# Another merge of five instruction streams, with 392 filler matmuls in place of 329, in a decoder layer in fp32

## The chip, the cores and the metric

The kernel runs on one NeuronCore of a Trainium2 chip. The metric is the device time of one execution in microseconds (us), as the median of several runs. One further execution was recorded by the hardware profiler; all rows below are from that one. Engines are named as the profile names them: PE is TensorE, DVE VectorE, ACT ScalarE, POOL GpSimd and SP SyncE. SP computes nothing here, it issues most of the DMAs.

## What is computed

Input `x` is 4 sequences of 512 tokens with 512 channels. Three residual blocks follow one another, each on a layer norm of its input:

```python
x = x + attention(layernorm(x), ...)                 # 16 query heads of 32, one shared key/value head, causal
x = x + quantised_mlp(layernorm(x), fside, ctx)      # two int8 "smooth quant" products with a silu gate between
x = x + ffn(layernorm(x), ...)                       # DFF 1376, shared LoRA, and 8 experts of LoRA rank 8, top 2 per token
```

The second block scales activations and weights by column maxima, rounds both to integers, multiplies, and undoes the scales; the first product is 512x512x512, the second 512x256x512. The third has a gate, an up and a down product. Accurate fp32 products are made of three matmuls on a high and a low part of each operand.

## The kernel before, in words

The work is cut into steps. Each step has a name and a place, such as `("max", b, g, i)`, where `b` is the sequence (0 to 3). Five generators list the steps in five streams:

- **A**, attention (`attention_steps`, from line 136): `turn1` transposes the normalised input; `kv`, `q` and `v` project; `rows` turns the row maxima of four heads; `scores`, `values`, `sums` and `context` are the softmax and its product with v; `out` projects.
- **X** (`maxima_steps`): 44 `max` groups for each sequence. PE computes scores with a causal mask into a PSUM bank (L1126 the mask, L1129 the scores), DVE reduces them to the negative row maximum (L1409). Groups 0 to 10 of four heads are: one of 4 heads x 128 columns, two of 2 x 256, four of 1 x 384, four of 1 x 512.
- **L** (`layer_steps`): the quantised block and the layer norms around it. DVE takes column maxima (L1459, L1474), scales (L1506), and takes row maxima (L1512); POOL scales the weights (L803); PE transposes and multiplies.
- **F** (`feed_forward_steps`): `turn3`, `low_in`, `router`, and then for each of 11 column tiles `gate`, `up`, `hid`, and by segments of tiles `ad` and `down`. It is the largest part of PE's work: L1056, L1057 and L1058 are the three matmuls of an accurate product.
- **W** (`preparation_steps`): once at the start, the shared LoRA is folded into the weights of the third block, tile by tile. `prep_gu` multiplies a fold of 8 rows on PE (L1066), DVE adds it (L1357), ACT rounds to the high part (L849), POOL takes the low part (L730); `prep_dn` is the same for the down weights (L1073, L1364, L855, L735). `prep_out(f)` on SP stores tile f and loads the raw weights of tile f+2 (L586 to L592). `gu_first` and the first `dn_load` fetch the prepared tiles, when all are stored.

A string, `TURNS`, merges the streams: each letter takes the next step of that stream, and a digit n is a `fill` of n matmuls. Inside a stream the order is fixed; only the merge is free. Every engine, SP among them, walks through the same merged list and issues its own part of each step (`for name, *where in ORDER`). So the order in the list is the order on all five queues, and each of them is strictly in order: an instruction that waits holds back all that is behind it on its queue. SP's queue carries, in the order of the list, the 8 + 1 transfers of each `q` step (L638, L642), the two transfers of each `rows` step (L649), which bring the row maxima to where `scores` reads them, the stores and loads of `prep_out`, and the loads of weights (`w_load`, L676: the weights of the quantised block).

A fill does no useful work:

```python
def fill(n):
    ps = in_ring.upcoming(pe)
    for _ in range(n):
        pe.matmul(ps[:, 0:2 * P], ident_bf[:, 0, :], ident_bf[:, :, :].to_broadcast([P, 2, P]), start=True, stop=True, ...)
```

It multiplies 128x128 by 128x256 in bf16 (L1053) into the one of the two `ring` banks that is to be used next, when that is free, and nobody reads the result. Banks of PSUM are handed out in the order of the list (`tenants_of`), four of them in rotation as `slots` and two as `ring`.

Of the kernel before, what the change touches and what calls it, by code (L numbers as in the profile page):

```python
# [303 lines left out]


TURNS = (
    "AAAAAAAAA6AAAAAAWAAX2X1WX9XXXXAXXXXXXAXWXXX3XWXXXW6XX91AXAAXXAAAXXAAAA1AAWXAAWXAAAAAW4A2AWXWXX5AWXXXAAAXXAXXXA"
    "XXAAAAAAAWXAAAAWAAAAAA79AAAAWAAAWAAA4AAAAAWAAAWAAAAAAA99AAAAAAAAAWAAAWAAAAAAAALALA2L5ALWLLLL5AWALAALLLWL15XXXX"
    "93LL1XXLXXLLLXLLLAXAWLXL995AWXXXXLXLLL9AAAXXXX4XLLLLXXAALXLLLWXXLLL31ALLALAXWAALXXL8AALAAAA1XW9LLLWXLAALAAAXL8"
    "XLAAXLAAALAL9AAXAAAXLLXLAAX94XLLLWLLWLLAWLLLAALXAXLXXLXAAAAAA2W8ALAAAAAAWALLLAAAAALWAALLAAWAAF6FALAAAAFAAAFAAA"  # L310
    "ALFWWWALAFAAALLLFAFAAFALLAALAFFAFFFFLAALLAFAAFFFXFXFLXLXXFLFFFFFFFLXFXAFFXXXFFFXXXFFFLFFFFFFFLXXFFLLLXLFXFF2FF"
    "FFAFFFFFLFFLFLXFXALLLFAFLXFXXFFALLFFLFFXAXLLLAXFFLFFXFALFFFLAFFLFFAFLFFFLLFLFLFXFLLLLAFFFLLXFFAFAALFLFFFFLAAXF"
    "FXXFXXFFLAFAXXFFFFFFFAXFALLFFLFFXFXXFLFFXFFFAFFLFAALLFAFFAAFLAFFFFLLAFAFAFFFFAAAAAALAFLFLAFAXFXFLLFXLAALFAFFAL"
    "AFLFAFLXAFLLLFFAFALFFAFFAALLFLAAFLAAFFFAFAFFLFFAAFLALFALFFALFFFFAAAAAFFLAAFFAAAAAFAAFAAAAFFFFLLAAFAFLAFFLAAAFF"
    "LLFLLFFFFFFFAFFFFFFAALFFFFLAAFFALAAFXFXXFFXXFLFFLFXFFXXFFFLFXXXFXAFFXXAFFFXFFLLLFFFFAFFFAXXFFFLLLFFFXXFFXXFFXL"
    "FFXFFXLLFLAFLXLLLFXAFFFFFAFFFLFLALFLAAAAFAALLFXFFFFLAALFLALFLAALAAFAAALFXFLLFLFFLFLFLLXFXLFFFFLLFFFLFFFFFFFLFF"
    "FLFLXLFFFLFLLXLLXAAFLFXFFFLFFFLLFFFFAFLXFXFXFLLFFXFFFXLFXFLFLFFFFLLXLFFFLFALLLFAFAALFFAXAFFXFFFAALLLFALFXFFLFF"
    "ALLLLFFAAAFFAFFFFAAAFAAFLLLFFFLFAAAFFFFFFFFAFFAAFFFAAFFFAAAAAAFFAAAAFAFFFAAAFAFLLLFAAFAAAAAFFAFAAFFFAAFAFAFAAF"
    "FAFFAFFFFFFFFFAFFFFFLLFFLFFLFFFLFFFLLFLFFFF9FFFLLFLF4LLFFFFFLFLFFFLFFLFFLFFFLLLFFFFLFFFLFFFLFFFLLFFLLFFFFFLLLL"
    "FFFFLFLLFFFLLFFLFFLFLFFFLLLFFFLFLFFFFFFFFLFLLFFFFLFLFLLLFFFFLLFLFFFFFLLFFFFFLFLFFLFFFLFFLLFLLFFFFLFLLLLFLFFFFF"  # L320
    "FFFFFLFFLLFLFFFFLFFFLFLLLLFFFFFFFFFFFFFFFFFFFFFFFF4F94F5FFFFF7FFFFFFFFFFFFFFFFFFFFFFFFFF994FFFFFFFFFFFFFFFFFFF"
    "F94FFFFFFFFFFFFFFFFFFFFFFFFFFFFFFFFFFFFFFFFFFFFFLFFFFFFFFFFFFFFFFF94FFFFFFFFFFFFFFFFFFFFFFFFFFFFFFFLFFFFFFFFF9"
    "FFL4FFFFFFFFFFFFFFFFFFFFFFFFFFFFFFFFFFFFFFFFFFFFFFFLFFFLFFFFFF2FFFFFFFFF")
# [1405 lines left out]
```

How the kernel before makes its waits and increments, by code:

```python
    def __call__(self, ins):  # L60
        self.n += 1
        ins.then_inc(self.chain.sem, 1)
        self.eng.wait_ge(self.chain.sem, self.chain.at(self.b, self.n))
# [11 lines left out]
    def claim(self, eng, key, signal, value):  # L75
        first, width = bank_after(self.next, BANK_WIDTH.get(key[0], 1))
        assert self.table[key] == (first, width), key
        for bank in range(first, first + width):
            if bank in self.left and (bank == first or self.left[bank] != self.left[first]):
                eng.wait_ge(*self.left[bank])
        for bank in range(first, first + width):
            self.left[bank] = (signal.sem, value)
        self.next = first + width
        return self.banks[:, first:first + width, :]
# [8 lines left out]
    def claim(self, eng, key, signal, value):  # L93
        place = self.n % 2
        self.n += 1
        assert self.table[key] == place, key
        if place in self.left:
            eng.wait_ge(*self.left[place])
        self.left[place] = (signal.sem, value)
        return self.places[place]
# [1 line left out]
    def upcoming(self, eng):  # L102
        place = self.n % 2
        if place in self.left:
            eng.wait_ge(*self.left[place])
        return self.places[place]
# [472 lines left out]
            def prep_wo():  # L580
                sp.wait_ge(wo_lo.sem, KT)
                sp.dma_start(wo_parts, wo_first[:, :, :].bitcast(F32)).then_inc(wo_stored.sem, 16)
# [29 lines left out]
            def x_load(b):  # L612
                if b < BATCH:
                    sp.wait_ge(xT_ps.sem, xT_ps.at(b - 1, 2))
                    if b > 1:
```

## Time and profile before

| | |
|---|---|
| median of 3 runs | 943.83 us (941.45 to 944.6) |
| the profiled execution's own time | 943.11 us |
| its span from the first to the last instruction | 941.4 us |
| PE busy | 902.0 us, 96% of the span |
| DVE, ACT, POOL busy | 552.4, 338.5, 309.5 us |
| mean granted clock of TensorE | 0.976 of full speed |

A busy PE is not a PE at its peak: a fill counts as busy, and so does a matmul at half the clock. The granted clock is 1.00 when TensorE runs at 2.4 GHz and 0.50 at 1.2 GHz. The idle time before an instruction stands behind it with the instruction that ended it; idle time on an engine that is not the bound costs nothing.

### The profile page before, as it was taken

How to read it: one execution, taken by the hardware profiler on the slowest of the kernel's cores; microseconds unless marked ns; L12 is line 12 of the kernel's file. 1: busy time of each engine (PE TensorE's matmuls, PEld its weight loads, DVE VectorE, ACT ScalarE, POOL GpSimd, SP SyncE). 2: the span in 40 equal slices, each digit the busy share in tenths (PEclk: the TensorE clock that was granted, in tenths of full speed). 3: DMA queues.
4: the chain of work that ended last, by engine and by line, in shares of the span. 5: the costliest groups of instructions: out<-in, count | busy, mean ns of one | idle time of the engine just before them, and what ended most of it. 6: DMA issues, size and time to landing. Idle time of an engine off the chain costs nothing.

```text
span 941.4 us, 13548 instructions
## 1 busy us (share of the span) xinstructions
PE 902.0 (96%) x5191; PEld 667.7 (71%) x5191; DVE 552.4 (59%) x897; ACT 338.5 (36%) x577; POOL 309.5 (33%) x419
## 2 busy tenths in 40 slices
PE   3989998899999999999999999999999999999998
PEld 2756567655578886766688767766778778688886
...
GB/s 310 266 207 256 301 190 129 171 142 211 307 224 175 218 129 150 130 201 240 117 174 251 134 106 161 132 290 108 163 159 162 168 180 206 91 242 194 170 179 95
DMA packets 44964, 175.07 MB, mean 186 GB/s; under 512 B 7196, under 2 KB 10268, under 8 KB 34916
## 3 DMA queue, kind: packets, MB, share of 16 engines
...
## 4 chain that ended last, share of the span: by engine, by line
PE 84%; DVE 7%; SPq 3%; ACT 2%; issue 2%; DMA 2%; POOL 0%; ACTq 0%; DVEq 0%
PE ring L1056 13%; PE ring L1058 13%; PE ring L1057 13%; PE slots L1129 4%; PE slots L1146 4%; PE av L1164 4%; PE ring L1296 4%; PE den L1164 3%; PE slots L1056 3%; PE slots L1058 3%; PE slots L1057 3%; SPq L642 2%; PE slots L1233 2%; PE ring L1053 2%; PE slots L1126 2%
## 5 line engine op out<-in xcount | busy, mean ns | idle before, releaser
L815 POOL TENSOR_TENSOR hd_l<-hd,hd_h 128x512 fp32r<-128x512 f32 x44 | 58.3, 1324 | 298.3 <-ACT hd_h L1023 298.3
L1056 PE MATMUL ring<-xT_h,gu 128*128 128x512 f32 x352 | 142.2, 404 | 0.0
L1058 PE MATMUL ring<-xT_h,gu 128*128 128x512 f32 x352 | 137.6, 391 | 0.0
L1057 PE MATMUL ring<-xT_l,gu 128*128 128x512 f32 x352 | 137.6, 391 | 0.0
L1409 DVE TENSOR_REDUCE negm<-slots 128x1 f32<-128x384 f32 (+3 forms) x176 | 106.4, 636 | 43.5 <-PE slots L1129 42.0
L931 ACT ACTIVATE probs<-slots 128x512 f32<-128x512 f32 (+1 forms) x176 | 90.0, 560 | 91.5 <-PE slots L1146 91.2
L782 POOL TENSOR_SCALAR_AFFINE_SELECT probs<-probs 128x128 f32<-128x128 f32 (+2 forms) x176 | 61.9, 361 | 132.7 <-ACT probs L931 130.7
L1129 PE MATMUL slots<-kst,qst 97*128 97x128 f32 (+3 forms) x256 | 77.7, 374 | 0.0
L1056 PEld LDWEIGHTS ring<-xT_h,gu 128*128 128x128 f32 x352 | 66.3, 188 | 15.2 <-issue 3.3
L1019 ACT ACTIVATE gated<-ring 128x512 f32<-128x512 f32 x44 | 26.3, 597 | 140.1 <-PE ring L1296 136.2
L1058 PEld LDWEIGHTS ring<-xT_h,gu 128*128 128x128 f32 x352 | 66.1, 188 | 14.5
L1057 PEld LDWEIGHTS ring<-xT_l,gu 128*128 128x128 f32 x352 | 66.4, 189 | 11.5
L1651 DVE TENSOR_TENSOR total<-ring,total 128x512 f32<-128x512 f32 x60 | 41.1, 687 | 48.1 <-PE ring L1058 47.6
L1146 PE MATMUL slots<-qst,kst 99*128 99x512 f32 (+1 forms) x176 | 63.0, 425 | 6.2 <-DMA qst<-negm_hl 4.5
L1056 PE MATMUL ring<-dn,hd_h 128*128 128x512 f32 x168 | 67.4, 401 | 0.9 <-DVE total L1651 0.9
L1057 PE MATMUL ring<-dn,hd_h 128*128 128x512 f32 x168 | 65.6, 391 | 0.0
L1058 PE MATMUL ring<-dn,hd_l 128*128 128x512 f32 x168 | 65.6, 390 | 0.0
L1023 ACT ACTIVATE hd_h<-hd 128x512 fp32r<-128x512 f32 x44 | 27.8, 631 | 100.3 <-DVE hd L1617 100.1
L1606 DVE SCALAR_TENSOR_TENSOR gated<-gated,ring 128x512 f32<-128x512 f32 x44 | 30.0, 683 | 53.6 <-ACT gated L1019 53.5
L1617 DVE SCALAR_TENSOR_TENSOR hd<-gated,ring 128x512 f32<-128x512 f32 x44 | 30.2, 686 | 47.8 <-PE ring L1296 39.2
L1126 PE MATMUL slots<-mask_r 128*128 128x128 f32 (+2 forms) x176 | 52.0, 295 | 2.0 <-DMA qst<-qT_h 1.5
L1129 PEld LDWEIGHTS slots<-kst,qst 97*128 97x128 f32 x256 | 49.1, 213 | 4.8
...
## 6 DMA issues: line engine op xcount, KB each, us to landing
...
qst<-qT_h SPq DMA_DIRECT2D x128, 64.0 KB, 2.1
...
```

The lines of the kernel that those rows point to most:

```text
L782: pool.affine_select(probs[:, at:at + heads, 0:P], probs[:, at:at + heads, 0:P], [[0, heads], [1, P]], ALU.is_ge, 0.0, base=0, channel_mul ...
L815: pool.tensor_tensor(hd_l[:, i, :], hd[:, i, :], hd_h[:, i, :].bitcast(F32), ALU.subtract).then_inc(hd_lo.sem, 1)
L931: act.activation(probs[:, at:at + heads, 0:n], slot("scores", b, step, unit)[:, 0, 0:heads * n].rearrange("p (h n) -> p h n", n=n), ACT.Ex ...
L1056: pe.matmul(out_, w_hi_, m_hi_, start=start, stop=False, skip_group_check=True)
L1057: pe.matmul(out_, w_hi_, m_lo_, start=False, stop=False, skip_group_check=True)
L1058: return pe.matmul(out_, w_lo_, m_hi_, start=False, stop=stop, skip_group_check=True)
L1126: pe.matmul(diagonal, mask_r[:, 0, :], mask_r[:, 1:2, :].to_broadcast([P, heads, P]), start=True, stop=False, skip_group_check=True)
L1129: mm = pe.matmul(ps[:, 0, h * n:(h + 1) * n], qst[0:MROW, 4 * g + h0 + h, qt * P:(qt + 1) * P], kst[0:MROW, 0:n], start=False, stop=True, ...
L1146: pe.matmul(ps[:, 0, 0:heads * n].rearrange("p (h n) -> p h n", n=n), kst[0:MROW + 2, kt * P:(kt + 1) * P], qst[0:MROW + 2, 4 * g + h0:4 * ...
L1164: mm = pe.matmul(to[HD * c:HD * c + HD, kt * P:T], weights, probs[:, 4 * (step % 2) + c, 0:n], start=(kt == TT - 1), stop=(kt == 0), skip_ ...
L1409: dve.tensor_reduce(negm[:, h0:h0 + heads, qt], slot("max", b, g, i)[:, 0, 0:heads * n].rearrange("p (h n) -> p h n", n=n), AX.X, ALU.max, ...
L1651: dve.tensor_tensor(total[:, tt, :], ps, total[:, tt, :], ALU.add)\
```

## The change

Only the string is another. All 1772 steps stay, each stream keeps its own order, and every engine issues the same instructions except for the fills. The digits sum to 392 in place of 329, so 63 matmuls are added. The list as it stands in the program, cut to the part in which the first two sequences go through attention and the preparation is made (the lines that follow are changed in the same manner):

```diff
 TURNS = (
-    "AAAAAAAAA6AAAAAAWAAX2X1WX9XXXXAXXXXXXAXWXXX3XWXXXW6XX91AXAAXXAAAXXAAAA1AAWXAAWXAAAAAW4A2AWXWXX5AWXXXAAAXXAXXXA"
-    "XXAAAAAAAWXAAAAWAAAAAA79AAAAWAAAWAAA4AAAAAWAAAWAAAAAAA99AAAAAAAAAWAAAWAAAAAAAALALA2L5ALWLLLL5AWALAALLLWL15XXXX"
-    "93LL1XXLXXLLLXLLLAXAWLXL995AWXXXXLXLLL9AAAXXXX4XLLLLXXAALXLLLWXXLLL31ALLALAXWAALXXL8AALAAAA1XW9LLLWXLAALAAAXL8"
-    "XLAAXLAAALAL9AAXAAAXLLXLAAX94XLLLWLLWLLAWLLLAALXAXLXXLXAAAAAA2W8ALAAAAAAWALLLAAAAALWAALLAAWAAF6FALAAAAFAAAFAAA"
-    "ALFWWWALAFAAALLLFAFAAFALLAALAFFAFFFFLAALLAFAAFFFXFXFLXLXXFLFFFFFFFLXFXAFFXXXFFFXXXFFFLFFFFFFFLXXFFLLLXLFXFF2FF"
...
+    "AAAA4AAAAA4AAA6AAA2AW2AAXX9XXXWXXXXX3XXX4AXWXXXWXXXXWXXXXXX991AXXAXAAAAAXWAAAAAAAAXAWAAAAAXAX92AAAAAXXAAAAAXXA"
+    "WXXWAAAAWAXXXAAWAAXA3A9AAAAAAAAAAWAAAAAWAAAAAAAAAAW8AAAAAWAAAAAAAWAWAAAAAAWWALA5LLA5AL5LWWWLLAALLA3ALLL94X2XX1"
+    "LWWXXLXLXLLWXXLLXAXLX24X5XLX1L423LLAAL5LLXL9XLL928X9X92L6XLAWXXLLXLWLWLL5AL3ALLXLXAAAAAALWAAAL3AXA5XAXAAWLLA1L"
+    "LXXL93X3AAAAX6LXXAALLALLALXAL5AAAALLAXAALWXXLL71LLLLAL2ALLLXLLX3WLLLALAWXLWLAALX6WAAXA5X5FAAAAAFAFAAAA3FAA4AAA"
+    "AAAAAAAFFAAAAAAAAAAALLAFALAWWWALALFLLAAAFLLAAFLAFAFFLLAAFFALAAFXFFXXXFXFFFXFXXFLFXFXFFFLLXFFFLFAFLXXFX1LFFFAFFF"
...
```

What it does between some marks, counted in the two lists (`scores(0,0,0)` is the first score step of the first sequence, `out(b,0)` the first half of a sequence's output projection, `product0(0,0)` the first product of its quantised block):

| from | to | fills before | fills after |
|---|---|---|---|
| start | `scores(0,0,0)` | 37 | 53 |
| `scores(0,0,0)` | `out(0,0)` | 50 | 31 |
| `out(0,0)` | `product0(0,0)` | 67 | 114 |
| `product0(0,0)` | `out(1,0)` | 68 | 79 |
| `out(1,0)` | end | 107 | 115 |

The same steps that use PE stand between these marks in both lists, but for three moves across them: `max(0,2,1)` to `max(0,2,4)` stand ahead of `scores(0,0,0)` after the change and behind it before; and a few steps cross `product0(0,0)`. Within the marks, `prep_gu(1)` to `prep_gu(4)` come later: `prep_gu(4)` has 11 `scores` steps, 6 `values` steps, `prep_dn(4)` and `prep_gu(5)` between it and `out(0,0)` before, and `values(0,14)`, `prep_dn(4)`, `values(0,15)` and `prep_gu(5)` after. `w_load(0)` follows `prep_out(4)` on SP's queue in both. `prep_gu(6)` and `prep_gu(7)` come earlier: `prep_gu(7)` stands between `scale_w(0,0,0)` and `scale_w(0,0,1)`, the first two of the four pieces in which POOL scales the weights, and stood behind `turn_w(0,0)`. `wqkv_out`, two stores of 1.15 MB each on SP's queue, moves from ahead of `q(0,2)` to behind it.

## Rows read from the trace of the kernel before

**Rows 1.** Stretches of the run, us: busy time of each engine, granted clock, DMA.

```profile
core 0: us, PE busy (x) PEld busy (x) DVE busy (x) ACT busy (x) POOL busy (x), PEclk, DMA share, GB/s
0.00:57.00 57.00, 37.64 (x196) 28.24 (x196) 24.32 (x43) 19.63 (x31) 26.07 (x33) 0.94 0.78 257
57.00:123.00 66.00, 64.15 (x491) 37.84 (x491) 32.77 (x61) 35.64 (x66) 38.30 (x67) 0.85 0.79 287
123.00:263.90 140.90, 132.50 (x919) 88.41 (x915) 107.13 (x174) 69.56 (x117) 70.78 (x96) 0.94 0.56 192
263.90:941.40 677.50, 667.69 (x3592) 513.25 (x3591) 388.18 (x620) 213.65 (x363) 174.30 (x224) 1.00 0.47 169
```

**Rows 2.** The same view of the two longest stretches at half clock.

```profile
49.66:63.31 13.65, 10.07 (x50) 7.97 (x51) 3.51 (x7) 2.53 (x6) 4.49 (x7) 0.50 0.54 195
76.97:90.62 13.65, 13.65 (x66) 9.63 (x68) 8.66 (x15) 5.11 (x10) 6.88 (x11) 0.50 0.60 210
```

**Rows 3.** PE in order of time: start, duration, engine, line, operation, count, idle before.

```profile
47.46 0.83 PE L1053 MATMUL ring<-ident_bf 128*128 128x256 bf16 x6
...
51.49 2.36 PE L1053 MATMUL ring<-ident_bf 128*128 128x256 bf16 x10
56.94 0.80 PE L1146 MATMUL slots<-qst,kst 99*128 99x512 f32 x1 [3.10 <-DMA qst<-negm_hl]
```

**Rows 4.** SP's queue in order of time, up to the first transfer of row maxima.

```profile
49.34 5.02 SPq L642 DMA_DIRECT2D qst<-qT_h  x8
54.47 1.15 SPq L649 DMA_DIRECT2D qst<-negm_hl  x2
```

**Rows 5.** PE in order of time: starts of two kinds of max groups, at full clock.

```profile
34.18 0.37 PE L1126 MATMUL slots<-mask_r 128*128 128x256 f32 x1
...
34.62 0.28 PE L1053 MATMUL ring<-ident_bf 128*128 128x256 bf16 x1
...
36.40 0.23 PE L1126 MATMUL slots<-mask_r 128*128 128x128 f32 x1
...
36.69 0.22 PE L1126 MATMUL slots<-mask_r 128*128 128x128 f32 x1
```

**Rows 6.** Fills: the shortest, median and longest, and 16 in a row at full clock.

```profile
L1053 PE MATMUL ring<-ident_bf x329: 272/273/437, 18.4 to 934.8; 128*128 128x256 bf16 x165
```

```profile
98.14 1.92 PE L1053 MATMUL ring<-ident_bf 128*128 128x256 bf16 x16
```

**Rows 7.** PE's waits over the whole run, the longest line: total, times, longest.

```profile
PE slots L1083 <- ACT x_in L860: 14.2, 4, 13.6
```

**Rows 8.** POOL and DVE in order of time: scaling of weights, scaling of activations, low parts.

```profile
161.45 6.97 POOL L803 TENSOR_TENSOR w_raw<-w_raw,rows 128x512 f32<-128x512 f32 x4 [2.63 <-ACT rows L946]
```

```profile
161.69 2.13 DVE L1506 TENSOR_TENSOR xn<-xn,rows 128x1024 f32<-128x1024 f32 x1
...
164.80 1.26 DVE L1506 TENSOR_TENSOR xn<-xn,rows 128x1024 f32<-128x1024 f32 x1
...
172.00 1.21 DVE L1512 TENSOR_REDUCE qm<-w_raw 128x2 f32<-128x1024 f32 x1
```

```profile
98.56 2.91 POOL L730 TENSOR_TENSOR gu<-raw_gu,gu 128x1280 fp32r<-128x1280 f32 x1 [2.53 <-ACT gu L849]
```

**Rows 9.** The load of the quantised block's weights: fold, values, projection, issue, landing, use.

```profile
105.61 1.16 PE L1066 MATMUL ring<-fold 8*128 8x128 f32 x16
```

```profile
119.83 0.85 PE L1164 MATMUL av<-probs,v 128*32 128x384 f32 x8
...
122.97 0.50 PE L1056 MATMUL slots<-wo_h,hT_h 128*128 128x512 f32 x1
```

```profile
116.16 1.31 SPq L676 DMA_DIRECT2D w_raw<-w  x1
```

```profile
w_raw<-w SPq DMA_DIRECT2D x1, 1024.0 KB, 9.0
```

```profile
140.03 3.94 DVE L1459 TENSOR_REDUCE tile_max<-w_raw 128x256 f32<-128x1024 f32 x2
```

More of the change, by code:

```diff
@@ L312 @@
[L312 to L321, printed above, removed]
@@ L322 @@
-    "F94FFFFFFFFFFFFFFFFFFFFFFFFFFFFFFFFFFFFFFFFFFFFFLFFFFFFFFFFFFFFFFF94FFFFFFFFFFFFFFFFFFFFFFFFFFFFFFFLFFFFFFFFF9"
-    "FFL4FFFFFFFFFFFFFFFFFFFFFFFFFFFFFFFFFFFFFFFFFFFFFFFLFFFLFFFFFF2FFFFFFFFF")
+    "AAAA4AAAAA4AAA6AAA2AW2AAXX9XXXWXXXXX3XXX4AXWXXXWXXXXWXXXXXX991AXXAXAAAAAXWAAAAAAAAXAWAAAAAXAX92AAAAAXXAAAAAXXA"
+    "WXXWAAAAWAXXXAAWAAXA3A9AAAAAAAAAAWAAAAAWAAAAAAAAAAW8AAAAAWAAAAAAAWAWAAAAAAWWALA5LLA5AL5LWWWLLAALLA3ALLL94X2XX1"
+    "LWWXXLXLXLLWXXLLXAXLX24X5XLX1L423LLAAL5LLXL9XLL928X9X92L6XLAWXXLLXLWLWLL5AL3ALLXLXAAAAAALWAAAL3AXA5XAXAAWLLA1L"
@@ new lines @@
+    "LXXL93X3AAAAX6LXXAALLALLALXAL5AAAALLAXAALWXXLL71LLLLAL2ALLLXLLX3WLLLALAWXLWLAALX6WAAXA5X5FAAAAAFAFAAAA3FAA4AAA"
+    "AAAAAAAFFAAAAAAAAAAALLAFALAWWWALALFLAAAFLLAAFLAFAFFLLAAFFALAAFXFFXXXFXFFFXFXXFLFXFXFFFLLXFFFLFAFLXXFX1LFFFAFFF"
+    "FFFFXXFLXFXFLFFLFFLFFFFFFFLFFFLFFLLLLFAFFLFAFLFFLXAFLXFXFLLFLLXFAXXFFFFFLFLFFFLFFFLXFLFXFFALLAFXFFFLLLFLFAALFL"
+    "ALFFLAFLLAAFFALAXFAXLLFLFFAXALAFLXXLFFAFFAFLFXFAFXFXFAFAFLFFFAFLXFXXXFXFFAFAAFFXAAAALLAFFFFAFFFFAAFFALAFAFXFXF"
+    "AFAAFLFLAFAFFLLFFLLLFFFXFLLFLLFLFAFLALAFAAALALFAAAFFFAFAFFLAALAAFFFFFFAFLFLAALFLFAFAFFFAAFLFFAAAAAAFFAAAAAAFFF"
@@ new lines @@
+    "FAAAALAFFFFFALALLFAFLFFFLLLFFFAFFFFFAFFFFFFFFAAFLLAAAFFXFXFXFXXFFXFLFLLXXAFFFLFXFXFXFFFXLLFFFFXFFXFFAXFFFFFXLX"
+    "FLFFLXLFFAFFFFLLLFAFFFLLLFFLLFXFLXFFFLFFLFLLFFFAFALFLFFLXLFXFFFFFALLFXFFXFLFFLFFAAXFLLLLFLLAFFFXFFFFLFLALLFAAF"
+    "ALFAAXFFALFAFLFXF1FFLLFFFLFFLLFLLAFXFFFLFFLXLLXFFFFFLFFFFFLLXFFFXLXFALFAAALLLFLFLFLALXFLFFAFXXXFFLFFAAFFAFAFLF"
+    "FFFLFFAXAAFFFFFLAAAAFXXFXAXLFXLLAAAFFFFFAFFAFAFAAAFAAAFFFFAFFAAAFAAFAAFALAAFAFAAAFFFAFAAAFAFFAAFAFAAAFFFAAAFLA"
+    "AAFAFAAAFFFLLLLLLLFFFAFFFFAFLFFFFALFFFFFFFFFLLFFLFF2LFFLFLFFFL92F3FFFLFLLFFFFFFLLLFFFLLFFFLFFLLFFFFLFFLFFFLFLF"
@@ L326, in streams_of @@
+    "FFLFFFFLFLLFLFFLFLFFFFLFFLFLFLLFFFLLFLLFFLFLFFLFLFFFFFFFLFFFFLFFLLFFFLFLFFLLLFLFFFFLFFLFFFLLFFLFFLFFFFFFFLLLFF"
+    "LLFLFFFFLLFFLLFFFFFFFLFFFFFFFFFFFLFFFFLFFFFFLFFLFFFFLFFFLLLFFLFFLFFFFFF92FFF8FF7FFFFFFFFFFFFFLFFFFFFFFFL4FFFF9"
+    "94FFFFFFFFFFFFF594LLFFFFFFFFFFFFFFFFFFFFFFFFFFFFFFFFFFFFFFFFFFFFFFFFFFFFFFFFF4FFFFFLLFFFF9FFFFFFFFFFFFFFFFFFFF"
+    "FFFFFFFFFFFFFFFFFFFFF9FFFFFFFFFFFFFFFFFFFFFFFFFFFFFFFFFFFFFFFFFFFFFFFFFFFFFFF4FFFFF1FFFFFFFFF")
 def streams_of():
```

## The prediction

> **What bounds the kernel now.** I read the run in stretches first [rows 1]. From 263.9 us on PE is busy for 667.7 of 677.5 us at full clock: that part is bound by PE's own work, which the change does not touch, and a merge can win almost nothing there. What can be won lies ahead of it, and I cut that at two marks of the list. Up to 57 us PE is busy for 37.6 us only. From there to `out(0,0)` at 123 us it is busy for 64.2 of 66.0 us, but at a mean clock of 0.85. From 123 to 263.9 us it is busy for 132.5 of 140.9 us at 0.94, while DVE is busy for 107.1.
>
> So I read the clock next. A clock of 0.85 over 66.0 us is 0.15 x 66.0 = 9.9 us of full-rate work not done; 0.94 over 140.9 us is 8.5 us; up to 57 us it is 0.06 x 57 = 3.4 us. Two stretches of 13.65 us each at 1.2 GHz hold most of it [rows 2]. The first has PE busy for 10.1 us of it, so waits lie inside. The second has it busy for all 13.65 us: there half a clock is half of the work, and nothing else shares the blame. Ahead of the first, TensorE had issued 6 fills and little else, then stood in a wait [rows 3]. The waits themselves are few: the longest line of them holds 14.2 us, and 13.6 of it are one wait at the start [rows 7]. The losses ahead of 263.9 us are thus fills, low clock and waits, in a part that is tied by dependencies.
>
> The mark at 57 us is fixed by SP, not by PE. `scores(0,0,0)` waited 3.10 us for a transfer of row maxima [rows 3]. SP issued it at 54.47 us, directly behind eight transfers of q that took 5.02 us to issue [rows 4]. The list after the change has the same transfers on SP's queue ahead of it, so I expect `scores(0,0,0)` at 57 us again, within 1 us; the two stores of `wqkv_out` change places with one `q` step, and all of them stay ahead of the row maxima.
>
> **The change, part by part.** I count against the profiled execution, 943.11 us with a span of 941.4 us; the median of the runs is 0.7 us above it.
>
> Work ahead of the fixed mark. Four max groups move in front of `scores(0,0,0)`, where PE only had fills and a wait. A group of two heads takes 34.62 - 34.18 = 0.44 us from start to start, one of a single head 36.69 - 36.40 = 0.29 us [rows 5]. Two of each are 1.46 us that no longer have to be done behind the mark: **-1.5 us**. The bound on the good side is twice that, when they would have run at half clock behind it; on the bad side 0, should the 19 fills that now stand between them and the scores be late: at half clock ten fills took 2.36 us [rows 3], so 19 can take 4.3 us, against 2.1 at full clock.
>
> The fills. One fill by itself takes 0.27 us, 16 take 1.92 us, so each further one costs (1.92 - 0.27)/15 = 0.11 us [rows 6]. The 63 are worth 6.9 us if nothing hides them. Their places matter more. Ahead of the first mark there are 16 more: they stand in the wait for SP, 0. Between the marks there are 19 fewer, 2.1 us; they too stood mostly in waits, which come back unless other work is ready, and I take 0. From `out(0,0)` to `out(1,0)` there are 58 more, 6.4 us. What would hide them is the chain of the quantised block, which runs through DVE, and PE's idle time of 140.9 - 132.5 = 8.4 us [rows 1]. I take 0, between +6.4 us (all in PE's way) and a gain of 8.5 us (they keep the clock up throughout); the busy DVE is the nearest row. From `out(1,0)` on there are 8 more in a part where PE is the bound: **+0.9 us**.
>
> The clock between the marks. 9.9 us are at stake [rows 1, 2]. The first low stretch began in the wait ahead of the mark; now five max groups and 19 fills keep PE issuing through that wait. The second stretch came in a mixture of thin prep folds, waits and few max groups; the folds of tiles 1 to 4 now stand later. They do not vanish, and with 19 fills fewer there the clock can fall at another place. I take 6 of the 9.9 us: **-6.0 us**, between 0 and -9.9. In the Trainium skill, TensorE: Matmul & The Clock Gate, section Terms, the penalty of throttled time is that time multiplied by the share of the clock that is missing. By that alone the term would be -9.9 us and the whole sum 3.9 us lower; I hold it for an upper end, because the first of the two stretches here contains waits that no clock shortens.
>
> POOL in the quantised block. `prep_gu(7)` now stands between the first and the second piece of POOL's scaling of the weights. Its low part takes 2.91 us [rows 8]. What is queued behind it on POOL are three scaling pieces, and DVE's row maxima of the weights wait for the last of them. In the trace POOL was done with all four at 161.45 + 6.97 = 168.4 us and DVE came to them at 172.0 [rows 8]: 3.6 us of slack, so 2.91 us fit, barely. But DVE multiplies the activations in the same place. That took 2.13 us while POOL was scaling, and 1.26 us the second time [rows 8]. I put **+1.0 us** for one more such collision on a busy DVE; its bounds are 0 and the 2.9 us for which POOL works. The Trainium skill, SBUF — State Buffer, section SBUF: two separate sides, says that a DVE operation with two inputs from SBUF and a GpSimd operation exclude each other for the whole instruction. By that rule the term would be 2.9 us and the sum 1.9 us higher; the row shows one multiplication longer by 0.87 us.
>
> The load of the weights. `prep_gu(4)` stood at 105.61 us, 17.4 us ahead of `out(0,0)`, and the load that follows its tile on SP was issued at 116.16 us, 10.6 us behind it [rows 9]. After the change `prep_gu(4)` itself, two `values` steps and two more folds lie between. The same two `values` steps took 122.97 - 119.83 = 3.1 us, and a fold 1.16 us [rows 9]: 3.1 + 3 x 1.16 = 6.6 us. The load is then issued 4 us behind the start of `out(0,0)` and, with 9.0 us to land, there at +13. DVE asked for it at 140.03, which is +17 [rows 9]. So 4 us of slack are left of 15; I charge 0, up to 3 us if the transfers of the tiles around it crowd it.
>
> Sum: -1.5 + 0.9 - 6.0 + 1.0 = **-5.6 us**. From the median of 943.83 us that is **938.2 us**. The steps after 263.9 us are merged in another order too; their waits in the trace are so small that I charge nothing for it, within 3 us either way.
>
> **The rivals.** A difference of 0.3%, 2.8 us, is about what a measurement of this kernel tells from none.
>
> First, the clock falls again. Nothing in the trace says that the new mixture between the marks is dense enough: the stretch that fell at 76.97 us was full of instructions, and the fills that could help are 19 fewer. Then -1.5 + 0.9 + 1.0 remains: 944.2 us, no difference. Against it stands the first stretch, whose cause is a plain wait that is now filled. Chance 0.18.
>
> Second, slower: the 58 fills between `out(0,0)` and `out(1,0)` are in PE's way. PE takes them in order, so a fill that starts when the chain's next matmul is ready delays the chain, then DVE, then the next sequence. It decides from the point at which less than their 6.4 us of PE's time there would have been idle. For it: 47 of them stand ahead of `product0(0,0)`, where DVE had hardly an idle gap; against it: PE's 8.4 us of idle time and 8.5 us of lost clock in that stretch [rows 1]. With the clock not regained between the marks it gives 944.2 + 6.4 = 950.6 us; with it, 944.6. The first is the rival: chance 0.26.
>
> Third, more than I take: both parts keep their clock. Then all 9.9 and 8.5 us are regained, with -1.5, +0.9 and +1.0: 943.83 - 18.0 = 925.8 us. It needs fills at every gap of the quantised block's chain, and DVE not to be the bound there, against 107.1 us of DVE in 140.9. Chance 0.10.
>
> That the change does not do what it says is no rival with a price: the fills are plain instructions and all of them are issued.
>
> **The numbers.** The forecast has 0.46: 938.2 us. The range reaches down to the third rival, with little behind it, and up to the second: 926 to 951 us. The forecast alone has 932 to 943. Faster by over 0.3% gets the forecast's larger part and the third rival, 0.52; within 0.3% the first rival and the forecast's upper end, 0.21; slower 0.27.
>
> **What would show it.** Right: the wait for the row maxima ends at 57 us within 1; `out(0,0)` starts between 114 and 118 us in place of 123; the mean clock between the marks is over 0.92; from `out(0,0)` to `out(1,0)` it takes 140 to 143 us; from there to the end 678 to 679. Wrong: a stretch of over 10 us at half clock behind 57 us (first rival); more than 146 us from `out(0,0)` to `out(1,0)` with PE busy throughout (second); a wait of DVE for the weights, or of the row maxima for POOL's scaling (my terms of POOL and of the load). If the time after `out(1,0)` differs by more than 3 us, what I left out of the sum was what mattered.

## The result, and the profile after

| | before | after |
|---|---|---|
| median (15 runs each, same chip) | 940.99 us (938.32 to 944.6) | 937.65 us (931.4 to 942.42) |
| ratio of the times, 95% interval | | 0.995 [0.9933, 0.9967] |
| profiled execution: its time, its span | 943.11, 941.4 us | 942.42, 940.7 us |
| PE busy | 902.0 us | 909.0 us |
| mean granted clock | 0.976 | 0.980 |

The change makes the kernel faster by 0.5%, 3.3 us between the medians. The profiled execution of after is the slowest of its 15, and its mean clock is one of the two lowest: the 15 lie between 0.980 (942.42 us) and 0.992 (934.47 us), and the fastest two, 931.4 and 931.74 us, had 0.989 and 0.991. Of one and the same list, how long TensorE stays at half clock differs between executions, so a stretch of one profile is a single sample.

The same stretches as in [rows 1], between the same marks, which now stand at 58.1, 110.8 and 258.9 us (columns as there), and behind them the longest stretch at half clock:

```profile
0.00:58.10 58.10, 45.15 (x222) 33.40 (x222) 26.64 (x47) 19.63 (x31) 26.03 (x33) 0.91 0.78 252
58.10:110.80 52.70, 52.00 (x463) 27.94 (x461) 29.42 (x57) 34.22 (x65) 35.69 (x64) 1.00 0.80 294
110.80:258.90 148.10, 140.15 (x974) 93.15 (x974) 104.79 (x173) 70.01 (x118) 73.03 (x98) 0.93 0.62 210
258.90:940.70 681.80, 671.68 (x3597) 515.96 (x3599) 385.73 (x621) 214.32 (x364) 173.98 (x226) 0.99 0.48 167
170.60:187.70 17.10, 16.77 (x68) 10.05 (x67) 7.24 (x10) 6.78 (x6) 5.66 (x4) 0.50 0.56 189
```

Against [rows 1] the four stretches are +1.1, -13.3, +7.2 and +4.3 us, together -0.7. So the part between the first two marks won 13.3 us where 7.5 were forecast (6.0 of clock and 1.5 of max groups), and the other three gave back all but 0.7. The second line has no half clock left at all: 0.15 x 66.0 = 9.9 us of lost full-rate work became 0.

At the first mark PE looks like this (PE in order of time, as [rows 3]); SP's queue stands under it:

```profile
53.79 0.63 PE L1129 MATMUL slots<-kst,qst 97*128 97x384 f32 x1
54.22 4.08 PE L1053 MATMUL ring<-ident_bf 128*128 128x256 bf16 x19
58.05 0.47 PE L1146 MATMUL slots<-qst,kst 99*128 99x512 f32 x1
```

```profile
46.84 8.58 SPq L642 DMA_DIRECT2D qst<-qT_h  x8
55.53 1.15 SPq L649 DMA_DIRECT2D qst<-negm_hl  x2
```

The wait of 3.10 us is filled by 19 fills, though the clock is at half there (19 in 4.08 us), as it was before. The eight transfers began 2.5 us earlier and took 8.58 us to issue, not 5.02 [rows 4]. `scores(0,0,0)` starts 2.52 us behind the issue of the row maxima (before: 2.47 us), and without a wait: as far as the rows tell, the transfer and the fills are done at about the same time. In head_only, a kernel of the experiments with the same list up to here, the maxima were issued at 54.01 us and the scores came 3.70 us later, directly behind the fills. There the fills at half clock set the mark, and no longer SP:

```profile
54.01 1.15 SPq L649 DMA_DIRECT2D qst<-negm_hl  x2
```

```profile
53.78 4.23 PE L1053 MATMUL ring<-ident_bf 128*128 128x256 bf16 x19
57.71 0.53 PE L1146 MATMUL slots<-qst,kst 99*128 99x512 f32 x1
```

Where the middle gave time back, PE stood behind DVE at the first `turn_a`, and the clock fell right behind it:

```profile
165.93 1.38 PE L1053 MATMUL ring<-ident_bf 128*128 128x256 bf16 x11
169.39 1.05 PE L1205 MATMUL slots<-ident_bf,a_bf 128*128 128x128 bf16 x16 [2.08 <-DVE negm L1409]
170.28 1.17 PE L1053 MATMUL ring<-ident_bf 128*128 128x256 bf16 x6
```

17.1 us at half clock are 8.5 us of work. The wait itself is not new. Before, PE stood just as long for DVE's row maxima at the place where the clock fell in this part (at half for 6.8 us from 172.5 us on):

```profile
172.23 0.27 PE L1136 MATMUL slots<-cst,negm 128*16 128x128 f32 x1 [2.24 <-DVE negm L1409]
```

Behind `out(1,0)` one new wait stands out, for a transfer of prepared weights, and the clock was at half for 6.8 us around its end; PE was busy for 5.9 of them (3.0 us lost):

```profile
304.67 0.28 PE L1053 MATMUL ring<-ident_bf 128*128 128x256 bf16 x1
307.97 0.77 PE L1056 MATMUL ring<-xT_h,gu 128*128 128x512 f32 x1 [3.02 <-DMA gu<-gu_parts]
```

3.02 + 3.0 = 6.0 us is more than the 4.3 us by which this stretch grew.

POOL and DVE at the place of [rows 8]:

```profile
154.36 3.72 POOL L730 TENSOR_TENSOR gu<-raw_gu,gu 128x1280 fp32r<-128x1280 f32 x1 [1.43 <-ACT gu L849]
158.03 3.72 POOL L803 TENSOR_TENSOR w_raw<-w_raw,rows 128x512 f32<-128x512 f32 x3
```

```profile
154.09 1.21 DVE L1506 TENSOR_TENSOR xn<-xn,rows 128x1024 f32<-128x1024 f32 x1
162.12 1.19 DVE L1512 TENSOR_REDUCE qm<-w_raw 128x2 f32<-128x1024 f32 x1
```

POOL was done at 161.75 and DVE came at 162.12 us: no wait, with 0.4 us to spare.

### The profile page after: what moved, and what is told of

Same layout as the page of the kernel before. It is cut to its first block, busy times and chain, and to the rows that moved or that the text cites. A ratio compares the mean times of both kernels' runs of the same rounds, so it can differ in the third digit from the quotient of the medians.

```text
span 940.7 us, 13665 instructions
## 1 busy us (share of the span) xinstructions
PE 909.0 (97%) x5246; PEld 670.4 (71%) x5254; DVE 546.6 (58%) x897; ACT 338.2 (36%) x577; POOL 308.7 (33%) x419
## 4 chain that ended last, share of the span: by engine, by line
PE 86%; DVE 5%; ACT 3%; DMA 2%; ACTq 2%; issue 1%; POOL 0%; SPq 0%; DVEq 0%
PE ring L1056 13%; PE ring L1057 13%; PE ring L1058 13%; PE slots L1129 4%; PE ring L1296 4%; PE av L1164 4%; PE slots L1146 4%; PE slots L1056 4%; PE slots L1058 4%; PE slots L1057 4%; PE den L1164 3%; PE ring L1053 3%; PE slots L1233 2%; PE slots L1126 2%; ACTq L913 2%; DMA gu<-gu_parts 1%
## 5 line engine op out<-in xcount | busy, mean ns | idle before, releaser
L1058 PE MATMUL ring<-xT_h,gu 128*128 128x512 f32 x352 | 138.6, 394 | 0.0
L1129 PE MATMUL slots<-kst,qst 97*128 97x128 f32 (+3 forms) x256 | 74.6, 358 | 0.0
L1053 PE MATMUL ring<-ident_bf 128*128 128x256 bf16 x392 | 56.8, 287 | 8.0 <-ACT mask_r L829 7.5
L1146 PE MATMUL slots<-qst,kst 99*128 99x512 f32 (+1 forms) x176 | 61.0, 405 | 1.1 <-DVE negm L1409 0.8
L1053 PEld LDWEIGHTS ring<-ident_bf 128*128 128x128 bf16 x392 | 36.4, 102 | 22.8 <-issue 7.6
```

What stands on the lines that cost most here:

```text
L1058: return pe.matmul(out_, w_lo_, m_hi_, start=False, stop=stop, skip_group_check=True)
L1129: mm = pe.matmul(ps[:, 0, h * n:(h + 1) * n], qst[0:MROW, 4 * g + h0 + h, qt * P:(qt + 1) * P], kst[0:MROW, 0:n], start=False, stop=True, ...
L1146: pe.matmul(ps[:, 0, 0:heads * n].rearrange("p (h n) -> p h n", n=n), kst[0:MROW + 2, kt * P:(kt + 1) * P], qst[0:MROW + 2, 4 * g + h0:4 * ...
```

## The experiments

All kernels keep the 1772 steps and the order inside each stream; only the string differs. B is the string of before, A that of after, and `[i:j]` a piece of it. The two lists have the same steps behind them at `out(0,0)` (187 characters of B, 186 of A) and at `out(1,0)` (465 and 482), so they can be cut and joined there. Ratios are against before, run on the same chip.

### The three parts alone

**head_only**: after's order up to `out(0,0)`.

```diff
-TURNS = B
+TURNS = A[:186] + B[187:]
```

> The list after the change up to out(0,0), the list before it from there on. My theory: the gain is made ahead of out(0,0), where the two profiles differ by 12.2 us, by clock (mean 0.99 in place of 0.85 between the marks) and by the work moved in front. Then this kernel keeps it and is faster than the full change: 8 to 12 us under the kernel before, ratio 0.987 to 0.992, out(0,0) at 109 to 113 us. Rival, luck of the clock: the low stretches fall elsewhere in each execution and the merge has no part in it; then it is within 3 us of the kernel before. Rival, the part behind absorbs it: out(0,0) is early, and the chain behind ends at the same time; then out(1,0) stands at 261 to 264 us and the total within 3 us.

Measured: 930.34 us (925.86 to 932.37), ratio 0.9869 [0.9834, 0.9904].

**mid_only**: after's order from `out(0,0)` to `out(1,0)`. (The text below says 61 fills more; there are 58.)

```diff
-TURNS = B
+TURNS = B[:187] + A[186:482] + B[465:]
```

> The list after the change from out(0,0) to out(1,0) alone, 61 fills more than the kernel before has there (the 58 of the table and 3 behind the seam by the way the digits were cut: at most 58 by count). My theory: this part costs, as the profile after shows (148.1 us in place of 140.9), so 4 to 8 us slower, ratio 1.004 to 1.009. Rival, the loss there was only one long low stretch of the clock that happened in the one profiled execution: within 2 us of the kernel before.

Measured: 951.41 us (948.26 to 953.55), ratio 1.0093 [1.0058, 1.0128].

**tail_only**: after's order from `out(1,0)` on.

```diff
-TURNS = B
+TURNS = B[:465] + A[482:]
```

> The list after the change from out(1,0) to the end alone, 8 fills more. Theory: the 8 fills cost 0.9 us and the late gate/up weights 3.0 us of wait and 3.4 us of low clock behind it: 1 to 6 us slower, ratio 1.001 to 1.006. Rival, the late weights come from the state in which the changed part before leaves the queues: then 0 to 1 us slower.

Measured: 949.31 us (944.59 to 953.49), ratio 1.0079 [1.0055, 1.0104].

The head wins 11.1 us against the 941.47 us of before beside it, three times the whole change: the theory for it holds, and both rivals fall (`out(1,0)` stands at 251.3 us, not at 261 to 264). The other two parts cost 9.9 and 7.8 us when they stand alone. For the middle that is the theory, a little above the upper edge of its range, and not one long low stretch of one execution. For the tail it is more than both expectations; its cause is another than the late weights (see below). The sum of the three is +6.6 us, the whole is -3.3: the parts do not add.

### What in the head wins

**start_only** and **between_only** cut the head at `scores(0,0,0)`. The four max groups are kept in the list once: in start_only they leave their old places, in between_only they stand in a row behind the mark.

```diff
-TURNS = B
+TURNS = A[:63] + B[56:187] less its first four X + B[187:]     # start_only
+TURNS = B[:56] + "XXXX" + A[63:186] + B[187:]                  # between_only
```

> The list of after up to and with scores(0,0,0) (four more max groups ahead of it, 53 fills in place of 37), the list of before from there on, less those four groups; 345 fills. head_only, which has after's list up to out(0,0), measured 0.987, with out(0,0) at 110.5 us against 123.0. Theory A, the part between the marks holds the larger share (the thin folds of the preparation among the scores let the clock fall at 77 us, and they are back here): the low stretch behind 57 us returns, out(0,0) starts at 118 to 122 us, time 936 to 940 us, ratio 0.995 to 0.999. Rival B, the filled wait ahead of the mark holds it (what TensorE did ahead of scores(0,0,0) decides for the scores behind it): no low stretch of more than 7 us between 58 us and out(0,0), which starts at 110 to 113 us, ratio 0.986 to 0.989.

Measured: 941.36 us (937.53 to 946.95), ratio 0.9996 [0.9971, 1.0022].

> The complement of start_only: before's list up to and with scores(0,0,0), then the four max groups max(0,2,1) to max(0,2,4) in a row, then after's list up to out(0,0), and before's behind it; 310 fills. Theory A: the low stretch behind 57 us goes, the one ahead of it stays at 10 to 14 us; out(0,0) at 112 to 115 us, time 931 to 935 us, ratio 0.989 to 0.993. Rival B: the mixture behind the mark changes nothing by itself, the clock falls behind 57 us for 10 us or more, out(0,0) at 120 to 123 us, ratio 0.998 to 1.002. If the two parts each give all of it, the losses are one and the same and either edit ends them.

Measured: 933.09 us (930.58 to 936.62), ratio 0.99 [0.9872, 0.9928].

Theory A holds in both, though start_only gained even less than it said: almost all of the head's gain comes from behind the mark. (In its profiled execution `out(0,0)` of start_only stands at 118.5 us, 4.5 us ahead of before's; the part behind `out(1,0)` took 680.2 us there, against 677.5, and the ratio shows no gain.) The stretch from `scores(0,0,0)` to `out(0,0)` in the two (columns as in rows 1), start_only first, with its low stretch under it, then between_only:

```profile
56.30:118.50 62.20, 59.27 (x482) 32.85 (x480) 30.00 (x57) 35.66 (x66) 38.27 (x67) 0.92 0.82 294
72.30:82.50 10.20, 10.20 (x49) 6.68 (x47) 5.47 (x9) 3.26 (x6) 7.13 (x8) 0.50 0.65 215
```

```profile
58.60:113.40 54.80, 54.05 (x474) 29.40 (x471) 31.50 (x61) 34.27 (x65) 35.73 (x64) 1.00 0.73 268
```

The low stretch at 72 us returns with before's order and is absent with after's, whatever TensorE did ahead of the mark.

**folds_early** puts back one thing between the marks, the places of the preparation's 14 steps (W):

```diff
-AXXAXAAAAAXWAAAAAAAAXAWAAAAAXAX92AAAAAXXAAAAAXXAWXXWAAAAWAXXXAAWAAXA3A9AAAAAAAAAAWAAAAAWAAAAAAAAAAW8AAAAAWAAAAAAAWAWAAAAAAWW
+AXXAXAAAAAXAAAAAWAAWAXAAAAWAAWWXAWX92AAAAAXXAAAAAXXAXXAWAAAAWXXXAAAAXA3A9AAAAWAAAWAAAAAAAAWAAAWAAAAAAA8AAAAAAAAAWAAAWAAAAAAA
```

> head_only with one thing undone: between scores(0,0,0) and out(0,0) the 14 steps of the preparation (folds and their stores) stand again where before has them, counted in attention steps (the first behind the 12th, not the 7th for the store; prep_gu(1) behind the 14th in place of the 33rd), the 31 fills and the max groups stay as in head_only; 326 fills. between_only measured 0.990, start_only 1.000, so the gain lies between these marks. Theory A, the forecast's: the thin folds among the scores let the clock fall, and later places keep it. Then a low stretch of 7 to 14 us returns between 60 and 100 us, out(0,0) starts at 115 to 119 us, time 935 to 939 us, ratio 0.993 to 0.997. Rival B: the places of the folds carry nothing; the 19 fills fewer and the max groups spread among the scores do. Then out(0,0) at 110 to 112 us, ratio 0.985 to 0.989.

Measured: 938.76 us (936.61 to 942.57), ratio 0.9963 [0.9943, 0.9984]. Of the head's 1.31%, 0.94 points are gone with this alone. The stretch between the marks, and PE where the clock fell:

```profile
57.60:121.90 64.30, 60.26 (x461) 32.11 (x462) 30.04 (x57) 36.02 (x66) 38.44 (x67) 0.87 0.83 301
```

```profile
68.98 1.12 PE L1073 MATMUL ring<-fold 8*128 8x512 f32 x2
70.03 0.51 PE L1146 MATMUL slots<-qst,kst 99*128 99x512 f32 x1
72.07 2.08 PE L1066 MATMUL ring<-fold 8*128 8x128 f32 x16 [1.53 <-DVE raw_dn L1364]
74.08 0.47 PE L1126 MATMUL slots<-mask_r 128*128 128x128 f32 x1
74.35 0.73 PE L1129 MATMUL slots<-kst,qst 97*128 97x512 f32 x1
74.88 0.63 PE L1146 MATMUL slots<-qst,kst 99*128 99x512 f32 x1
75.44 2.07 PE L1073 MATMUL ring<-fold 8*128 8x512 f32 x2
```

Theory A again. The places of the folds carry it, and by two ways. Folds close to one another need the same `ring` banks and the same DVE, so PE waits for the addition of the last fold (1.53 us, `raw_dn`). And around that wait stand folds of 8 rows; the clock falls for 10.2 us, and the same fold takes 2.08 in place of 1.16 us. Two more falls of 3.4 us each stand in this stretch, at 99.3 us with no long wait ahead (0.41 us) and at 113 us behind a wait of 2.06 us for POOL. Together the half clock is 8.5 us and the idle time 3.3 us more than in head_only, of 11.5 us by which the stretch is longer. What lowers the clock no run here separates. A wait is not needed for it: in after it fell at 47.7 us, behind a fold at 45.17 us, with PE busy for 9.52 of the 9.72 us ahead. In start_only and in before a fold had also waited for `raw_dn`, 0.63 us, ahead of the fall at 72.3 and 76.97 us; between the marks of head_only and after no fold waits for it.

**fills_back**: after's order between the marks with before's 50 fills in place of 31.

```diff
-AXXAXAAAAAXWAAAAAAAAXAWAAAAAXAX92AAAAAXXAAAAAXXAWXXWAAAAWAXXXAAWAAXA3A9AAAAAAAAAAWAAAAAWAAAAAAAAAAW8AAAAAWAAAAAAAWAWAAAAAAWW
+AXXAXAAAAAXWAAA1AAAAAXAWAAA4A2A5XAXAAAAAXXAAAAAXXAWXXWAAAAWAXXXAAWAAXAA79AAAAAAAAAA4WAAAAAWAAAAAAAAAA99WAAAAAWAAAAAAAWAWAAAAAAWW
```

> head_only with 50 fills in place of 31 between scores(0,0,0) and out(0,0), at the places that before has them by attention steps; every other step as in head_only; 345 fills in all. The forecast charged 0 for these 19 fills fewer. Theory A: they stood in waits, ratio as head_only, 0.985 to 0.989, out(0,0) at 110 to 111.5 us. Rival B: they stood in PE's way at 0.11 us each, 2.1 us: out(0,0) at 112 to 113.5 us, time 931.5 to 933.5 us, ratio 0.989 to 0.991. In between_only and before the stretch differs by 11.3 us, of which 6.8 is clock by the profile, so B is the likelier by that remainder.

Measured: 932.97 us (929.33 to 935.17), ratio 0.9895 [0.9868, 0.9922]. The median lies in rival B's range and `out(0,0)`, at 111.5 us, at the edge of theory A's; the interval overlaps head_only's, so the medians alone do not decide. The profile shows the stretch, which has clock 1.00 in both kernels. fills_back first, then head_only:

```profile
57.40:111.50 54.10, 53.94 (x480) 29.84 (x480) 29.52 (x57) 34.44 (x65) 35.80 (x64) 1.00 0.79 286
```

```profile
57.70:110.50 52.80, 52.10 (x464) 28.05 (x462) 29.47 (x57) 34.26 (x65) 35.79 (x64) 1.00 0.81 293
```

19 fills more are 1.84 us more of busy PE and 1.3 us more of time: some two thirds of their price is in PE's way, and the rest stood in waits. Each theory had a part of it.

### Where the middle loses

**head_seam** adds to head_only the first 35 characters of the middle, **head_mid** all of it.

```diff
-TURNS = A[:186] + B[187:]
+TURNS = A[:221] + B[219:]     # head_seam
+TURNS = A[:482] + B[465:]     # head_mid
```

> head_only with one more piece of after's list: the steps from out(0,0) to max(1,0,2), in which prep_dn(5) and prep_gu(6) stand ahead of the projections of the second sequence, and 29 fills in place of 18 or so. In after it took 31.4 us from out(0,0) to turn(0,0), 26.5 us in head_only and before. Theory A, this seam is where after gives back time: turn(0,0) 4 to 6 us later than in head_only and nothing of it made up behind it, time 934 to 937 us, ratio 0.991 to 0.995. Rival B, the loss is made up because the chain of the quantised block is what sets product0(0,0), by DVE: turn(0,0) late but product0(0,0) within 2 us of head_only's 176.0, ratio 0.986 to 0.989.

Measured: 930.42 us (929.52 to 931.23), ratio 0.9868 [0.9842, 0.9893], the same as head_only. `turn(0,0)` came 31.4 us behind `out(0,0)`, 4.9 us later than the 26.5 us in head_only, but `product0(0,0)` came 66.5 us behind it against 65.5. Theory A falls: the lateness is made up, as rival B has it, where the chain through DVE and not PE's work sets `product0(0,0)`. Part of it is clock: from `out(0,0)` to `product0(0,0)` the mean is 0.95 in head_seam and 0.92 in head_only. The seam has a close pair of folds of its own, with a wait of 1.60 us for `raw_dn` in head_seam and in after, and 3.4 us of half clock behind it.

> The list of after up to out(1,0), that of before from there on; 384 fills. The three parts alone measured -11.1 (head), +9.9 (middle) and +7.8 us (tail), +6.6 together, where the whole change measured -3.3. If parts simply add, this one is at -1.2 us: 940 us, ratio 0.999, and adding after's tail to it would have to GAIN 2 us though it costs 7.8 us by itself. Theory A, the tail costs nothing of its own behind after's middle (its price in tail_only came at the seam and in one wait of 5.2 us that after does not have): 936 to 939 us, ratio 0.994 to 0.998, from out(1,0) to the end within 2 us of 677.5. Rival B, the tail always costs: after's tail behind it is worth 5 us or more, and this is at 930 to 933 us, ratio 0.988 to 0.992, with out(1,0) to the end 4 us shorter than in after.

Measured: 936.35 us (935.15 to 937.48), ratio 0.9928 [0.9902, 0.9955]. By the ratios the middle costs 0.0059, 5.6 us, behind after's head, and since head_seam costs nothing, it does so behind the seam. What after's tail adds to head_mid is 0.0022, 2 us, with overlapping intervals, far from tail_only's 0.0079. The ratio lies between the ranges of theory A and rival B and its interval reaches into both; simple addition (0.999) is excluded. From `out(1,0)` on it took 680.2 us, 1.6 less than in after: nearer to theory A (within 2 us of 677.5) than to rival B (4 us shorter than in after).

**mid_less_fills** is head_mid with before's number of fills from `out(0,0)` to `product0(0,0)`, 67 in place of 114, taken from the longest; the piece behind `turn(0,0)`:

```diff
-LLL94X2XX1LWWXXLXLXLLWXXLLXAXLX24X5XLX1L423LLAAL5LLXL9XLL928X9X92L6XLAWXXLLXLWLW
+LLL44X2XX1LWWXXLXLXLLWXXLLXAXLX24X4XLX1L323LLAAL3LLXL3XLL323X3X32L3XLAWXXLLXLWLW
```

> head_mid (after's list up to out(1,0), before's behind it; 0.993) with 67 fills in place of 114 between out(0,0) and product0(0,0), the number that before has there, taken from the longest ones; 337 in all. head_mid is 5.9 us slower than head_only, with 58 fills more and another order between out(0,0) and out(1,0). Theory A (the forecast's second rival): the fills are in PE's way. Then 47 x 0.11 = 5.2 us come back: out(0,0) to product0(0,0) 65 us in place of 69.4, time 930 to 932 us, ratio 0.986 to 0.989. Rival B: DVE's chain sets product0(0,0) (a wait of 2.09 us for a row maximum stands behind 48 of the fills), so PE stands idle where the fills were; out(0,0) to product0(0,0) stays at 68 to 70 us, ratio 0.991 to 0.994. Rival C: without them the clock falls for 10 us or more, and it is slower than head_mid, over 0.995.

Measured: 939.77 us (933.58 to 943.46), ratio 0.9967 [0.9942, 0.9992]. It came out slower than head_mid by 0.4%, though the intervals just overlap (head_mid's ends at 0.9955); it was certainly not 5 us faster. The stretch from `out(0,0)` to `out(1,0)`, first head_mid, then mid_less_fills with its low stretch:

```profile
110.20:255.60 145.40, 136.90 (x974) 91.83 (x974) 104.67 (x173) 69.98 (x118) 73.29 (x98) 0.95 0.65 216
```

```profile
110.30:258.00 147.70, 135.78 (x927) 89.28 (x927) 104.74 (x173) 69.98 (x118) 73.01 (x98) 0.92 0.63 212
166.00:186.50 20.50, 17.84 (x81) 11.62 (x83) 10.47 (x16) 9.76 (x11) 5.04 (x4) 0.50 0.61 191
```

Half clock costs half of PE's busy time in it. head_mid had four stretches of 3.4 us there, PE busy throughout, 6.8 us lost; mid_less_fills had 3.4 + 20.5, with 21.2 us busy, 10.6 us lost. Taken off, the two need 138.6 and 137.1 us, and head_only (140.8 us with 17.1 at half clock) 132.3. By this estimate the 47 fills stand in PE's way for 1.5 us, and they pay for it: without them PE is idle for 11.9 us in place of 8.5, it waits longer for the same row maxima ahead of `turn_a(0,0)`, 2.74 in place of 2.09 us, and more is lost to the clock. One profile each would not show the last, but all executions do for the whole run: the median of the mean clocks is 0.982 without them (12 executions) and 0.988 with them (6). Rival C is what happened, theory A's mechanism is in it, and neither number of fills makes this order as good as before's.

```profile
164.87 0.72 PE L1053 MATMUL ring<-ident_bf 128*128 128x256 bf16 x5
168.33 0.91 PE L1205 MATMUL slots<-ident_bf,a_bf 128*128 128x128 bf16 x7 [2.74 <-DVE negm L1409]
```

**after_no_fills**: after with all 392 fills left out.

```diff
-TURNS = A
+TURNS = A less its digits
```

> The list after the change with all 392 fills left out. If the fills mostly stand in PE's idle time and hold the clock: 5 to 20 us slower than the change, with a mean clock under 0.96. If they are in PE's way (the slower rival of the prediction): up to 6 us faster than the change. If neither: within 2 us of the change.

Measured: 945.11 us (937.92 to 951.95), ratio 1.0033 [1.0001, 1.0066], 0.8 points behind after, with mean clocks of 0.946 to 0.958: the first of the three readings. From `out(0,0)` to `out(1,0)`, then the last part from `rank(1,0)`:

```profile
114.30:267.10 152.80, 134.65 (x782) 85.81 (x780) 105.89 (x173) 70.56 (x118) 70.44 (x98) 0.81 0.61 209
668.00:943.60 275.60, 263.09 (x1236) 206.51 (x1234) 126.24 (x197) 63.01 (x101) 57.47 (x57) 1.00 0.47 171
```

In the middle the clock is 0.81 without fills, 0.93 with them; in the last part it is 1.00 either way, and that part takes 280.6 us in after (from 660.1 us), 5.0 us more with 113 fills in it. Fills are worth something in the one place and cost something in the other.

### The tail, and why parts don't add

tail_only has one wait that no kernel with after's whole list has. PE and DVE around it:

```profile
466.32 0.39 PE L1058 MATMUL slots<-wo_h,hT_l 128*128 128x512 f32 x1
471.95 0.77 PE L1056 MATMUL slots<-wo_h,hT_h 128*128 128x512 f32 x1 [5.24 <-issue]
```

```profile
467.49 2.63 DVE L1589 TENSOR_TENSOR wx<-prob,wsum 128x256 f32<-128x256 f32 x2
470.04 0.68 DVE L1651 TENSOR_TENSOR total<-ring,total 128x512 f32<-128x512 f32 x1
470.64 1.21 DVE L1439 TENSOR_TENSOR x<-slots,x 128x1024 f32<-128x1024 f32 x1
```

The profile names no releaser ("issue"), but the program does. `out(2,1)` needs two PSUM banks side by side, and `bank_after` (L125) starts at bank 0 again if a pair does not fit into the four. Worked through for each list it gives:

```
                 out(2,0)    out(2,1)
before           2, 3        0, 1
after            0, 1        2, 3
tail_only        1, 2        0, 1
```

In tail_only the list in front leaves bank 1 as the next one. `out(2,0)` takes 1 and 2, bank 3 alone holds no pair, and `out(2,1)` starts at bank 0: it needs bank 1, which `out(2,0)` still holds. DVE reads that at L1439, behind the router's work of another sequence, and ends at 470.64 + 1.21 = 471.85 us. PE starts at 471.95. The clock was at half for 6.8 us from 469.1 us on, of which PE was busy for 3.95 us, 2.0 us lost. With the wait that is 7.2 us, most of the 7.8 us of tail_only. after's own tail behind after's middle has no such pair and costs some 2 us. No run moves the pair back, so this is argued and not tested; it rests on the program's own assignment, on 0.10 us between the end of the reader and the start of PE, and on its absence in after. mid_only changes the banks behind `out(1,0)` too, and took 681.3 us from there against 677.5, where its longest wait is 2.3 us for a transfer of row maxima, and head_only's is 1.4. It has a pair that wraps as well, `product0(2,0)` in banks 1 and 2 and `product1(2,0)` in 0 and 1, and so has head_mid; how much of that part of the price it is stays open.

### A faster version

**no_late_fills**: head_only without the fills behind `out(1,0)`.

```diff
-TURNS = A[:186] + B[187:]
+TURNS = A[:186] + B[187:465] + (B[465:] less its digits)
```

> head_only without the 107 fills that stand behind out(1,0), all but 2 of them behind out(3,0), where TensorE is the bound; 219 fills. In after_no_fills the stretch from rank(1,0) to the end took 271.5 us against 275.7 in before, with no fall of the clock in it. Theory A: each late fill costs its PE time only where nothing else was waited for, so 4 to 6 of 107 x 0.11 = 11.8 us come back: 924 to 927 us, ratio 0.980 to 0.984, the fastest of all. Rival B: they keep the clock up in the last sequence, where waits are frequent; a low stretch appears behind 790 us and the time is that of head_only or more, 930 to 934 us, ratio 0.987 to 0.991.

Measured: 925.73 us (925.12 to 926.97), ratio 0.9825 [0.9799, 0.985]. Theory A. From `rank(1,0)` to the end, head_only first:

```profile
649.90:929.60 279.70, 271.44 (x1323) 215.32 (x1321) 127.02 (x197) 62.37 (x98) 53.54 (x54) 1.00 0.47 169
```

```profile
648.40:923.50 275.10, 261.95 (x1216) 206.74 (x1216) 127.00 (x197) 62.32 (x98) 53.53 (x54) 0.99 0.48 172
```

107 fills less are 9.5 us less of busy PE and 4.6 us less of time; a short stretch of half clock appears at 788 us, about where rival B put one, and takes 1.7 us. It beats before by 1.75%, and after too: 0.9825 [0.9799, 0.985] against 0.995 [0.9933, 0.9967], each measured against before.

## Why the prediction was right, and by which steps it was not

The time was forecast at 938.2 us and the median is 937.65. Against before on the same chip the gain is 3.3 us where 5.6 were forecast. That the total is so near is luck. By stretches of the profiled execution the forecast was 0, -7.5, +1.0 and +0.9 us, and +1.1, -13.3, +7.2 and +4.3 were measured: a gain that was put too small and two losses that were put too small cancel. `out(0,0)` stands at 110.8 us and not between 114 and 118.

**The mark at 57 us** came at 58.1, just outside the 1 us given. That SP sets it holds for before. After the change the fills end at the same time as the transfer, and in head_only they end later. That SP's transfers take the same time was wrong (8.58 for 5.02 us to issue).

**The clock between the marks, -6.0 us of 9.9.** The mechanism was right: the thin folds standing later is what did it (between_only, folds_early), and the clock there is 1.00. The size was the upper end: all 9.9 us. The rule of the Trainium skill (TensorE: Matmul & The Clock Gate, section Terms), which the forecast weighed and held for too high, gives it to within what the stretch shows. My reason against it was that the first stretch holds waits. They lie ahead of the mark; the 6.3 us of that stretch behind the mark (3.2 us lost) have PE busy throughout, as has the second one at 77 us (6.8 us lost). The cause that I gave for the first stretch, a plain wait that is now filled, was wrong: the wait of 3.10 us began only after the clock had fallen at 49.66 us (one of 1.50 us for a transfer of q stood around the fall), and with it filled the clock still is at half from 47.7 to 58.0 us. It merely ends at the mark, and ahead of it costs little, as far as PE would else have waited for SP.

**The four max groups, -1.5 us.** Plausible in the profile, since the groups stand where fills stood, but start_only as a whole measured 0.9996 [0.9971, 1.0022]; 1.5 us alone can't be told from none.

**The 19 fills fewer between the marks, 0.** "They too stood mostly in waits" was wrong: 1.3 us by the profile of fills_back. 9.9 + 1.5 + 1.3 to 2.1 is 12.7 to 13.5, and 13.3 us were won; PE's idle time in the stretch fell by 1.2 us too, so the agreement is not exact.

**The stretch from `out(0,0)` to `out(1,0)`: the 58 fills, 0.** Here the sum failed most: the stretch took 148.1 us in after and 145.4 in head_mid, where 140 to 143 were said. Both mechanisms that I had set against each other are there at once: the fills are in PE's way (second rival), and they hold up a clock that falls lower without them (third rival's condition). But the fills are not the whole of it. With before's number of fills ahead of `product0(0,0)` (mid_less_fills) the new order still took 147.7 us, against 140.8 with before's order (head_only). For this order I had taken no term. No run puts after's fills into before's order, so how the loss divides between the two stays open, and so does what in the order costs: the wait of 2.08 us for row maxima ahead of `turn_a(0,0)` is no longer than the one of 2.24 us at 172.23 us in before.

**POOL, +1.0 us.** The collision came at another place and cost nothing that can be seen. POOL's slack of 3.6 us shrank to 0.4, but held. DVE's multiplication was not longer (1.21 us); POOL's low part was, 3.72 in place of 2.91 us. They overlapped from 154.36 to 155.30 us, and 3.72 - 2.91 = 0.81 us is nearly that overlap. DVE had started first, POOL paid, and POOL had time. The Trainium skill (SBUF — State Buffer, section SBUF: two separate sides) says that the one that starts first holds the shared port and the other waits; the trace agrees. In [rows 8] it was POOL that had started first (161.45 against 161.69 us) and DVE that took longer. The direction agrees there too, the size less well: of the first of POOL's four pieces (6.97 us together) some 1.5 us were left by my estimate, and DVE grew by 0.87 us.

**The load of the weights, 0.** Right. It was issued at 114.41 us, 3.6 us behind `out(0,0)` (forecast 4); DVE came to it at 130.50, 19.7 us behind that mark, without a wait.

**From `out(1,0)` to the end**, 678 to 679 us were said and 681.8 measured. That is 4.3 us more than before, over the 3 us from which, by the forecast's own sign, what was left out of the sum is what mattered. The 8 fills more are 0.9 us of it. after has one wait for prepared weights at 307.97 us, with the half clock around it. But head_mid, with before's tail and without that wait, took 680.2 us as well, so this wait is not all of it. The range of 3 us either way for "merged in another order" was too narrow for a single wait of that size, and the reason that I gave for it, that the waits of before are small there, says nothing of another order.

**The first rival** (the clock falls again, 944.2 us) needed a low stretch of over 10 us between the first two marks. There is none. The sign that I gave, such a stretch anywhere behind 57 us, was too wide: there is one of 17.1 us behind `out(0,0)`.

**The second rival as a whole** (slower, 950.6 us) needed the head to win nothing. Its sign, more than 146 us from `out(0,0)` to `out(1,0)`, came, but with PE idle for 8.0 of the 148.1 us. mid_only shows that its other half was no fancy: after's middle behind before's head is 1.0093 [1.0058, 1.0128].
